# Expert weights as the stationary operand: a filled buffer for each pair, turns of eight

## What is computed

```python
router_logits_BTE = jnp.einsum('BTD,DE->BTE', x, kernel_router_DE)
weights_BTX, indices_BTX = jax.lax.top_k(softmax(router_logits_BTE), 2)
norm_weights_BTX = softmax(weights_BTX)
gating_BTEF = jnp.einsum('BTD,EDF->BTEF', x, kernel_gating_EDF)
fuse_BTEF   = silu(gating_BTEF) * jnp.einsum('BTD,EDF->BTEF', x, kernel_up_EDF)
down_BTED   = jnp.einsum('BTEF,EFD->BTED', fuse_BTEF, kernel_down_EFD)
out_BTD     = jnp.einsum('BTED,BTE->BTD', down_BTED, full_weights_BTE)
```

## Time and profile before

| | us |
|---|---|
| median of 3 runs (806.3 to 811.54) | 810.86 |
| the profiled execution | 808.4 |
| its span, first to last instruction | 806.2 |
| first gate-up matmul | 507.5 |
| last gate-up starts | 758.7 |
| last scatter starts | 770.7 |
| first load of the result is issued | 772.9 |

### The profile page before, as it was taken

The page is one execution under the profiler, slowest core; times in us unless marked ns, Lnnn a source line. Parts: engine busy times, 40 slices in busy tenths (PEclk is TensorE's granted clock), DMA queues, the critical chain, the costliest instruction groups (busy, mean ns, idle before and its releaser), DMA issues. The chain is left out here.

```text
span 806.2 us, 15721 instructions
## 1 busy us (share of the span) xinstructions
PE 641.9 (80%) x3781; PEld 541.0 (67%) x3783; DVE 592.4 (73%) x1430; ACT 468.7 (58%) x1030; POOL 408.6 (51%) x609
## 2 busy tenths in 40 slices
PE   0695628989999999999999987798888888897900
PEld 0694316777777777777777776687777777786700
DVE  7787899988888988888878987455555555554445
ACT  0452437787887878788778864455554555554400
POOL 3000007666676766767657676155555555555520
PEclk9999999999999999999989999899999999999965
DMA  9970100000000000000000033133233332332169
GB/s 307 260 152 0 29 0 22 23 29 23 23 28 22 28 21 21 25 24 25 22 24 22 26 104 116 47 94 94 86 93 95 96 90 86 95 96 76 52 240 385
DMA packets 57800, 62.52 MB, mean 78 GB/s; under 512 B 9545, under 2 KB 48848, under 8 KB 57777
## 3 DMA queue, kind: packets, MB, share of 16 engines
q1 hardware_dynamic: 49072, 45.19, 19.7%
q0 software_dynamic: 8704, 17.06, 6.2%
HBM read 30.73 MB, written 32.54 MB: 78 GB/s over the span
## 5 line engine op out<-in xcount | busy, mean ns | idle before, releaser
L446 POOL DMA_INDIRECT moe_d<-raw,slot_st x144 | 141.5, 983 | 130.2 <-issue 107.2
L419 POOL DMA_INDIRECT slots_d<-rows,slot_st x128 | 135.5, 1058 | 73.8 <-POOL rows L414 52.5
L1030 DVE SCALAR_TENSOR_TENSOR act<-raw,taps,act 128x512 f32<-128x512 f32 x192 | 149.1, 784 | 21.8 <-ACT act L510 20.9
L1223 DVE CAST x_hi<-bank 128x256 fp32r<-128x256 f32 x72 | 30.6, 425 | 100.3 <-PE bank L861 82.9
L395 POOL TENSOR_TENSOR xde<-xb,e_end 128x256 f32<-128x256 f32 x64 | 45.8, 716 | 113.6 <-DVE xb L1107 112.0
L854 PE MATMUL bank<-xw_hi,x_hi 128*128 x144 | 64.3, 447 | 29.8 <-DVE x_lo L1225 29.4
L771 PE MATMUL bank<-xb,m_sb 128*128 128x64 f32 x512 | 75.4, 297 | 4.6 <-POOL xde L395 4.3
L880 PE MATMUL bank<-act,raw 128*128 x576 | 76.7, 276 | 1.7 <-issue 1.2
L771 PEld LDWEIGHTS bank<-xb,m_sb 128*128 128x128 f32 x512 | 72.6, 215 | 6.4 <-issue 4.6
L661 ACT ACTIVATE raw<-bank 128x256 f32<-128x256 f32 x72 | 28.1, 390 | 80.4 <-remote 70.1
L880 PEld LDWEIGHTS bank<-act,raw 128*128 128x128 f32 x576 | 70.2, 192 | 2.8 <-issue 2.8
(11 more groups left out here) (231 smaller groups left out, 1667.8 us busy)
## 6 DMA issues: line engine op xcount, KB each, us to landing
slots_d<-rows SPq DMA_DIRECT2D x8, 1188.0 KB, 14.3
rows<-slots_d SPq DMA_DIRECT2D x72, 132.0 KB
x_sb<-in_x SPq DMA_DIRECT2D x8, 512.0 KB, 7.5
act<-in_x SPq DMA_DIRECT2D x64, 64.0 KB
xw_hi<-moe_d SPq DMA_DIRECT2D x8, 512.0 KB, 9.1
xw_lo<-moe_d SPq DMA_DIRECT2D x8, 512.0 KB, 9.8
out<-x_sb SPq DMA_DIRECT2D x8, 512.0 KB, 13.5
moe_d<-raw,slot_st POOLq DMA_INDIRECT x144
```

The source lines that it names most:

```text
L419: nc.gpsimd.indirect_dma_start(out=slots_d, out_offset=bass.IndirectOffsetOnAxis(ap=slot_st[:, r, c:c + 1], axis=0), in_=rows[:, r, c, :], ...
L446: nc.gpsimd.indirect_dma_start(out=moe_d, out_offset=bass.IndirectOffsetOnAxis(ap=slot_st[:, r, c:c + 1], axis=0), in_=ym[r][:, c * D:(c + ...
L1030: V.scalar_tensor_tensor(out=group_act(par)[:, t, :], in0=proj[:, t, k:k + GT], scalar=taps[:, t, k:k + 1], in1=group_act(par)[:, t, :], o ...
```

## The change

Gate-up is turned round: the expert's weights are stationary, in pieces of 128 columns, and the 256 rows of the pair stream. These pieces are read at fixed addresses: SyncE copies each pair's weights (hi and lo, 4 KB in each of 128 partitions, 512 KB) from `gu` in SBUF to one of NW = 4 buffers `gu_w`, also in SBUF. h then comes out with features as rows, as `down` needs it, so `turn_h` and `hidden_keep` go; the token weight, now along the free dimension, is applied to the output in `y_keep`. A turn has U = 8 pairs, with eight places for rows, `ym` and `x_again`. TensorE and SyncE read eight expert numbers at a turn's start. The lags change: SyncE slot_load 0 and expert_load 4; TensorE gate_up 2, turn_x 0, down 4; VectorE x_keep 0, hidden 2, destination 4 (in this order, it was destination before hidden); ScalarE y_keep 5, silu 2. x transposes alternate between banks 0 and 6.

```diff
 R = 4
-TURN0, TURN1 = 2, MP // R
+U = 8
+TURN0, TURN1 = 2, MP // U
+NW = 4
...
-        ht = [raw[:, (2 * R + u * 4) * P:(2 * R + u * 4 + 4) * P] for u in range(2)]
+        ht = [act[:, 4096 + i * 2 * PS:4096 + (i + 1) * 2 * PS] for i in range(NW)]
-        gu_hi, gu_lo = xw_hi[:, 0:E * 2 * F], xw_lo[:, 0:E * 2 * F]
+        gu = xw_lo[:, 0:E * 4 * F].rearrange("p (e s n) -> p e s n", e=E, s=2)
+        rows_m = xw_hi[:, 0:U * K * ROW].bitcast(F32).rearrange("p (r c v) -> p r c v", r=U, c=K)
+        gu_w = [xw_hi[:, 4096 + i * 4 * F:4096 + (i + 1) * 4 * F] for i in range(NW)]
...
+            def sp_read_experts(m):
+
+                _, sp_experts[0] = nc.values_load_multi_w_load_instructions(
+                    eid[0:1, bass.ds(m * U, U)], engines=[nc.sync.engine], min_val=0, max_val=E - 1,
...
             def slot_load(m, r):
                 if not is_first(m):
-                    sp.wait_ge(id_done, (m - 1) * R + r + 1)
-                sp.dma_start(rows[:, r, :, :], slots_d[bass.ds((m * R + r) * PS, PS), :]
+                    sp.wait_ge(id_done, (m - 1) * U + r + 1)
+                sp.dma_start(rows_m[:, r, :, :], slots_d[bass.ds((m * U + r) * PS, PS), :]
...
+            def expert_load(m, r):
+
+                if is_first(m) and r < 1:
+                    sp.wait_ge(gu_lo_done, 1)
+                if not (is_first(m) and r < NW):
+                    sp.wait_ge(gu_done, m * U + r - NW + 1)
+                ex = sp_experts[0][(r + U // 2) % U]
+                sp.dma_start(gu_w[r % NW].bitcast(F32), xw_lo[:, bass.ds(ex * (4 * F), 4 * F)].bitcast(F32))\
+                    .then_inc(ld_gu[r % NW], 16)
...
-            over_pairs(sp, [(slot_load, 0)], [load_again])
+            over_pairs(sp, [(slot_load, 0), (expert_load, 4)], [load_again], begin=sp_read_experts)
...
-                for c in range(2):
-                    a = A(l_sb[:, r % 2, c * F:(c + 1) * F], bank[2 + 2 * (r % 2) + c][:, 0:F], ACT.Silu)
-                a.then_inc(silu_m, 1)
-
-            def hidden_keep(m, r):
-                act_e.wait_ge(ht_done, m * R + r + 1)
-                A(ht[r % 2], bank[6][:, :], ACT.Copy).then_inc(hts_done, 1)
...
+                A(l_sb[:, r % 2, :], bank[2 + 2 * (r % 2)][:, :], ACT.Silu).then_inc(silu_m, 1)
...
+                for c in range(2):
+                    y = A(ym[r][:, c * D:(c + 1) * D], bank[1 + 6 * (r % 2)][:, c * D:(c + 1) * D], ACT.Copy,
+                          scale=weight_m[:, r, c:c + 1])
+                y.then_inc(ym_done, 1)
...
             def gate_up(m, r):
 
-                ex = expert(m, r)
-                pe.wait_ge(xts_done, m * R + r + 1)
+                pe.wait_ge(ld_gu[r % NW], 16 * (m * (U // NW) + r // NW + 1))
+                pe.wait_ge(xts_done, m * U + r + 1)
+                if not (is_first(m) and r < 2):
+                    pe.wait_ge(h_done, m * U + r - 1)
                 for c in range(2):
-                    for a, (xs, w) in enumerate(((x_hi, gu_hi), (x_hi, gu_lo), (x_lo, gu_hi))):
-                        gu = mm(bank[2 + 2 * (r % 2) + c][:, :], xs[:, r % 2, c * P:(c + 1) * P],
-                                w[:, bass.ds(ex * (2 * F), 2 * F)], start=(a == 0), stop=(a == 2))
-                gu.then_inc(gu_done, 1)
+                    for f in range(2):
+                        for a, (part, xs) in enumerate(((0, x_hi), (0, x_lo), (1, x_hi))):
+                            o = part * 2 * F + c * F + f * P
+                            g = mm(bank[2 + 2 * (r % 2) + c][:, f * PS:(f + 1) * PS], gu_w[r % NW][:, o:o + P],
+                                   xs[:, r % 2, :], start=(a == 0), stop=(a == 2))
+                g.then_inc(gu_done, 1)
...
-            over_pairs(pe, [(gate_up, 1), (turn_x, 0), (turn_h, 2), (down, 3)])
+            over_pairs(pe, [(gate_up, 2), (turn_x, 0), (down, 4)], begin=read_experts)
...
+            def hidden(m, r):
+
+                dve.wait_ge(silu_m, m * U + r + 1)
+                V.tensor_tensor(ht[r % NW], l_sb[:, r % 2, :], bank[3 + 2 * (r % 2)][:, :], ALU.mult)\
+                    .then_inc(h_done, 1)
...
             def destination(m, r):
                 if not is_first(m):
                     dve.wait_ge(st_moe[r], 16 * 2 * m)
-                V.tensor_copy(slot_st[:, r, :], rows[:, r, :, D]).then_inc(id_done, 1)
+                V.tensor_copy(weight_m[:, r, :], rows_m[:, r, :, D + 1])
+                V.tensor_copy(slot_m[:, r, :], rows_m[:, r, :, D]).then_inc(id_done, 1)
...
-            over_pairs(dve, [(x_keep, 0), (destination, 2), (hidden, 1)], [residual])
+            over_pairs(dve, [(x_keep, 0), (hidden, 2), (destination, 4)], [residual])
```

More of the change, by code:

```diff
@@ L134, in program @@
         slot_st = sb("slot_st", [P, R, K], I32)
+        slot_m = sb("slot_m", [P, U, K], I32)
+        weight_m = sb("weight_m", [P, U, K])
         w_ln = act[:, 0:DI + CONV]
@@ L177, in program @@
         scat = [sem(f"scat{i}") for i in range(R)]
-        ld_slot = [sem(f"ld_slot{i}") for i in range(R)]
-        st_moe = [sem(f"st_moe{i}") for i in range(R)]
-        ld_again = [sem(f"ld_again{i}") for i in range(R)]
+        ld_slot = [sem(f"ld_slot{i}") for i in range(U)]
+        ld_gu = [sem(f"ld_gu{i}") for i in range(NW)]
+        st_moe = [sem(f"st_moe{i}") for i in range(U)]
+        ld_again = [sem(f"ld_again{i}") for i in range(U)]
         ld_sum = [[sem(f"ld_sum{i}_{c}") for c in range(K)] for i in range(8)]
@@ L228, in over_sequences, with over_pairs @@
             body(NB - 1)
-        def over_pairs(eng, stages, beside=()):
+        def over_pairs(eng, stages, beside=(), begin=None):
             def turn(m, checked):
-                for r in range(R):
+                if begin:
+                    begin(m)
+                for r in range(U):
                     for fn, lag in stages:
-                        if not checked or 0 <= m * R + r - lag < MP:
-                            fn(m + (r - lag) // R, (r - lag) % R)
-                    if not checked:
+                        if not checked or 0 <= m * U + r - lag < MP:
+                            fn(m + (r - lag) // U, (r - lag) % U)
+                    if not isinstance(m, int) or TURN0 - 1 <= m < TURN1:
                         for fn in beside:
-                            fn(m - TURN0, r)
+                            fn(m - TURN0 + 1, r)
             lags = [lag for _, lag in stages]
-            assert (TURN1 - TURN0) * R == NT and 0 <= min(lags) and max(lags) <= R
+            assert (TURN1 - TURN0 + 1) * U == NT and 0 <= min(lags) and max(lags) <= U
             for m in range(TURN0):
@@ L247, in over_pairs @@
                 turn(m, False)
-            for m in range(TURN1, -(-(MP + max(lags)) // R)):
+            for m in range(TURN1, -(-(MP + max(lags)) // U)):
                 turn(m, True)
@@ L360, in _ @@
             chain(pool.memset(rows[:, :, :, :], 0.0))
+            chain(pool.memset(eid[:, :], 0))
             chain(pool.iota(tokid[:, 0:1], pattern=[[0, 1]], base=K * NT * P, channel_multiplier=1))
@@ L446, in moe_scatter @@
                     nc.gpsimd.indirect_dma_start(
-                        out=moe_d, out_offset=bass.IndirectOffsetOnAxis(ap=slot_st[:, r, c:c + 1], axis=0),
+                        out=moe_d, out_offset=bass.IndirectOffsetOnAxis(ap=slot_m[:, r, c:c + 1], axis=0),
                         in_=ym[r][:, c * D:(c + 1) * D], in_offset=None,
```

99 lines of the change are left out of this document (45 added, 54 removed).

## The result

| | before | after |
|---|---|---|
| median (4 runs each, us) | 811.2 | 834.94 |
| lowest to highest | 806.3 to 811.74 | 831.25 to 839.74 |
| the profiled execution | 808.4 | 831.25 |
| its span | 806.2 | 829.4 |
| first gate-up starts | 507.5 | 507.9 |

The change is slower: ratio 1.0318, interval 1.028 to 1.0356. All of it lies in the expert stage: the last scatter starts 22.9 us later, and the profiled execution ends 22.85 later.

A forecast was written before the change was run, and what follows sets the result against it. TensorE, 2.95 us a pair plus 0.61 of late-signal stall, was taken as the bound; afterwards a closed loop, 7.6 us for two pairs, moves the last scatter from 770.72 to 776.8: 808.4 + 6.1 = 814.5, said 815, range 786 to 850.

The forecast's parts named there:

- A: Expert stage: the forecast that a closed loop sets 3.6 to 4.05 us a pair, 802 to 831 us; chance 0.48.
- rival C: Expert stage: late TensorE signals remain if GpSimd's pause falls well under 2 us, or DMA is busier; 831 to 860, chance 0.24.
- The loop: Gate-up, VectorE's step, slot load, expert load, landing, gate-up two pairs on: 7.6 us for two pairs, 3.80 a pair.
- 256-column matmuls: TensorE's gate-up: 12 matmuls of 256 columns at 0.13 us each, 1.56 us a pair instead of 1.40.
- Landing: Expert load within SBUF: 512 KB lands in 3.0 us, between 2.84 and 3.76, the latter mostly a cold start.
- The start: Start of the expert stage: first gate-up stays at about 507.5, and gate-up 3 starts at 515.5.
- The sum: Expert stage added up: loop for pairs 4 to 67, last four at 2.8 us; last scatter at 776.8 against 770.72.
- my last sign of being wrong: TensorE: its clock falling in the idle time between gate-ups would show the forecast wrong; no size given.
- Rival B: Expert stage: a shorter loop, landing 2.45 us and matmuls at 0.11, 6.81 for two pairs; 790 us, chance 0.2.
- Rival D: Expert stage: no loop, weights always early, TensorE or GpSimd sets 2.8 us a pair; 752 us, chance 0.08.
- TensorE's saving: TensorE in the expert stage: dropping four h transposes saves 0.44 us; a pair takes 2.67 instead of 2.95.
- Expert numbers: TensorE and SyncE: 144 loads of about 0.30 us become one a turn on each; costed at nothing.

The follow-up runs named there:

- experiment 4: The changed kernel with expert loads only for the first four pairs, and no later load or wait for it; 818.09 us, ratio 1.0141 to the kernel before.
- 11: The kernel before the change, with TensorE's expert numbers read once a turn instead of two single reads a pair; 765.34 us, ratio 0.9946.
- experiment 1: The changed kernel with VectorE's destination and weight casts moved to the head of its step; 812.23 us, ratio 1.0066 to the kernel before.
- 6: Experiment 1's kernel with a GpSimd clear of 480 columns, waited for, behind each pair's two scatters; 825.2 us, ratio 1.0231 to the kernel before.
- 8: The kernel before the change, with a GpSimd clear of 480 columns, waited for, behind each pair's two scatters; 827.84 us, ratio 1.0269.
- 5: Experiment 1's kernel with GpSimd issuing one of each pair's two scatters; 756.28 us, ratio 0.9383 to the kernel before.
- 7: Experiment 1's kernel with two GpSimd clears of 480 columns, waited for, behind each pair's two scatters; 857.09 us, ratio 1.0616 to the kernel before.
- 9: Experiment 1's kernel with a GpSimd clear of one column, waited for, behind each pair's two scatters; 795.61 us, ratio 1.0352 to the kernel before.
- 10: The kernel before the change, with a GpSimd clear of one column, waited for, behind each pair's two scatters; 797.59 us, ratio 1.0388.
- 12: A repeat of 9: experiment 1's kernel with the one-column GpSimd clear behind each pair's scatters; 797.5 us, ratio 1.0367 to the kernel before.

## Why the prediction was right, and where it was off

The forecast was 815 by a closed loop (A), its own range 804 to 822, all of it 786 to 850. Measured are 831.25 in the profiled execution and 834.94 as the median: the mechanism of A as forecast, the size 16 to 20 us over it. The time is inside the whole range, outside A's own, and at the lower edge of rival C's 831 to 860. The sign was hardly called: 815 is +0.5%, measured are +3.2%, and slower had a chance of 0.38. That the wide range held is in part luck.

- **The loop** is there, with the members named and in their order. Its legs, from the rows at 648.26: silu after 1.70 (1.84 forecast), x_hi and x_lo to 2.72 (2.86), product to 3.31 (3.46), casts to 3.59 at the end of slot_m (3.69), slot load 3.78 and expert load 4.26 (4.45), landing to gate-up 3.39 (3.15 with its 0.15). Sum 7.65, forecast 7.6. Two errors cancel: the legs up to the expert load were 0.19 quicker, most of it the matmuls, and the landing 0.24 slower.
- **256-column matmuls**: from the first at 648.26 to the transposes at 649.76 are 1.50 us for 12, 0.125 each with the slower first one, against the 1.56 and 0.13 of the forecast. Behind the second one they step at 0.118 (648.46 to 649.64). The last four pairs take 2.51 to 2.61 us, and experiment 4's undisturbed ones 2.52, forecast 2.67 to 2.8.
- **Landing** 3.39 from issue, between my 2.84 and 3.76, with the slot load's 132 KB issued 0.48 us ahead on the same queue. I had put most of the 3.76 down to a cold start; no run shows one, and with the queue in use the landing is only 0.4 shorter. The fit of the Trainium skill ("DMA: Bandwidth & Descriptors", Anatomy of one DMA), which is for GpSimd's queue, gives an estimated 3.2 for this size; the row, of SyncE's queue, is 0.2 above it.
- **The start** held: gate-up 0 at 507.89 (507.5), gate-up 3 at 516.16 (515.5).
- **The sum is 16.8 us short** at the last scatter (793.6, forecast 776.8), and the step that failed is that of rival C taken as all or nothing. I gave held signals to C alone and none to A. Up to pair 60 there is hardly one (an x_hi 0.9 us late, at 523.87), behind it they are there. By term: start +0.7; the loop (7.66 - 7.6) x 32 = +1.9; pairs 3 to 28, 101.4 us where 25 x 3.83 is 95.7, +5.6; pairs 60 to 67, 29.6 where 26.8, +2.8; the last four pairs 10.2 where 11.2, -1.0; from the last gate-up to the last scatter 13.7 where 6.9, +6.8. The last term is held signals and the ten scatters queued behind them. So is the term for pairs 60 to 67. The term for pairs 3 to 28 is another one, the loop's legs taken as constant. Two landings that gate-up waited for were longer, 5.06 us (pair 8) and 4.29 (pair 19); the expert loads of 6, 11, 17, 25 and 26 were issued 4.8 to 5.2 us behind the gate-up two pairs before and not 4.3; and the granted clock was 0.57, 0.72 and 0.72 from 530 to 534, 540 to 546 and 597 to 603, partly the lower level, each time behind a stand of TensorE (2.81, 2.82 and 1.86 us ahead of the gate-ups at 529.39, 539.13 and 597.80). Such a fall was my last sign of being wrong; it covers 16 of the 101 us. What lengthened the two landings isn't known.
- **Rival C's point of decision** was right in kind: with GpSimd still for 1.5 to 1.6 us between pairs the signals are on time (C had it decided well under 2), and where two pairs bunch they are held.
- **Rival B** (shorter loop) didn't come: the matmuls, at 0.118 to 0.125, are nearer to A's 0.13 than to its 0.11, and the landing is 3.4 and not 2.45. **Rival D** (2.8 a pair, 752) came out at 2.85 and 756 once the loop was open *and* half the scatters gone; opening the loop alone gave 3.58. Its price in my text, with GpSimd's small gaps and no held signals, left out the second bound.
- **TensorE's saving** (2.95 to 2.52 a pair) is real and worth nothing here: first the loop, then the held signals stand before it.
- **Expert numbers.** Costed at nothing. Where signals are held this wasn't tested; without them the reads cost 4 us (11).

What isn't settled: what holds the signals, and why some chips do it and others don't. The change itself wasn't run on a chip that doesn't. There its loop should still take 3.83 us a pair, since nothing was held in the pairs where that was read; against 2.945 for the kernel before, it would lose more than here. That is an estimate.

## What to carry to other kernels

A copy into a ring of buffers is only prefetch if its issue depends on nothing recent: follow the queue's instruction order back to the last thing that each wait needs, and if the chain comes back to the consumer, divide its length by the pairs it spans. Moving one cheap instruction group ahead in an engine's step can change that span (here from two pairs to three, and 2.5% of the time). Before pricing a step as a gain, look for the bound just under the present one; taking the load away entirely showed it in a single run.

## What the runs showed of the hardware

- On some chips TensorE's semaphore signals are held while GpSimd issues four or more indirect DMAs in a row: by 1 to 3 us beside four (before), by up to 5.7 beside six (experiment 1, a silu at 679.50 behind matmuls that ended at 673.81). They are let go about 1 us after the last one (0.4 to 1.4 in the rows looked at). With 1.5 us between pairs of them (experiments 6 and 8) or 1.6 (the change) they were on time. That the scatters do it is read from experiments 5 to 8; how, no run shows. The kernel before showed it on the chip of its profile, and took 769 us and not 807 on those of experiments 9 to 12, where the profile of 11, nearly the same kernel, has none of it: 5% for an unchanged program. Compare only against a run on the same chip.
- A scatter that waits for a clear ahead of it on GpSimd starts 0.87 to 0.99 us behind it (experiments 6 to 10 and 12), one that follows another scatter 0.30: a one-column clear of 0.14 us with its wait costs 0.8. The wait for the semaphore wasn't taken apart from the clear.
- A copy of 512 KB within SBUF, 4096-byte pieces, took 3.4 us from issue to its first reader, 256 KB in 2048-byte pieces 2.7: about 0.7 us for the second 256 KB (an estimated 360 to 400 GB/s), and by a straight line through the two an estimated 2 us that don't depend on size.
- One read of an expert number took TensorE's sequencer 0.30 us, one load of eight 0.59:

```profile
L873 PEldq TENSOR_LOAD <-eid x10: 588/594/1413, 503.6 to 775.7; - x10
```
